# Five tables that interleave the expert blocks with routing and attention, replaced in a macaron layer kernel

## The chip, the core and the metric

One core of a Trainium2 chip. The engines of the core run their own instruction streams side by side: PE (TensorE), DVE (VectorE), ACT (ScalarE), POOL (GpSimd) and SP (SyncE, which only issues DMAs here); they meet at semaphores. The metric is the device time of one execution in microseconds (us), median of the runs.

## What is computed

A macaron layer over 4096 tokens of width 128: half a feed-forward part, windowed attention, and the same feed-forward part by half again, with the same weights both times.

```python
x = x + 0.5 * ffn(layernorm(x))
x = x + attn(layernorm(x))
x = x + 0.5 * ffn(layernorm(x))

def ffn(x):                      # 8 experts, 2 of them for each token, and a shared expert
    normed = layernorm(x) * ln_gamma + ln_beta
    logits = normed @ router_w.T                       # [4096, 8]
    top_v, top_i = top_k(softmax(logits), 2)
    comb = sum(one_hot(top_i) * softmax(top_v))
    for e in range(8):                                 # 2 x 384 hidden columns each
        out += comb[:, e] * swiglu(normed, gate_up_w[e], down_w[e])
    return out + swiglu(normed, shared_gate_up_w, shared_down_w)   # 128 hidden columns

def attn(x):                     # 32 windows of 128 tokens
    q, k, v = x @ Wq.T + bq, x @ Wk.T + bk, x @ Wv.T + bv
    scores = q @ k.T / sqrt(128)
    keep the 32 highest of each row, softmax, times v
    return layernorm(leaky_relu(out) + x) * gamma + beta
```

## The kernel before

The tokens are 32 tiles of 128, taken in 8 steps of 4 tiles. A step of routing is called R: R0 to R7 belong to the first feed-forward part, R8 to R15 to the second. A step of routing normalizes its tokens, forms the logits on PE (`turn_z`, `logits`), picks two experts for each token on DVE (`pick`, then `rows`, which works out a row number for each pair of token and expert), runs the shared expert (`shared_up`, `shared_down` on PE), and scatters every token twice into a list in HBM, sorted by expert (`scatter` on POOL, L1572).

The experts then work on blocks: 128 rows of that list that all belong to one expert. There are 163 blocks, B0 to B162. The lists of the first part come in three groups of 3, 3 and 2 steps (g0, g1, g2), those of the second in two, of 7 steps and 1 (g3, g4), and some groups are listed in several phases; the phases start at B0, B9, B31, B62, B85, B102, B118, B126 and B148. At the start of a phase SP waits for the scatters of all steps up to it. At the end of a group the lists are filled up with zero rows (`fill_all`, two batches of four DMAs at L499, and `fill_spare`). A block consists of parts:

- part 0: SP fetches the 128 rows into `xin` (L479), PE transposes them (L711), ACT writes `x_t` (L920), POOL copies the row numbers to `idx` (L1584);
- part 1: SP copies the expert's gate and up weights (L484), PE multiplies by the gate weights (L716), ACT applies silu (`sil`, L923);
- part 2: PE multiplies by the up weights (L721), DVE forms the product h (L1397);
- part 3: PE multiplies by the down weights (L730), ACT copies (L929), POOL scatters the rows to `results` in HBM (L1589).

Part 4, eight times at the start, transposes the weights of one expert (PE L692). SP reads the row and weight offsets of four blocks at a time into registers (L441). The text writes B83.3 for part 3 of block 83, and h47 for the product of block 47 on DVE.

After the blocks of a group, each of its steps is combined: SP loads the two results of each token (`results(C, ...)`, L515), DVE adds them (`combine`, L1297). With C0 to C7, attention works on the sums of a step: DVE searches for the 32 highest scores (`search`, L1370), forms the `probabilities` (L1385, from ACT's `exps`), PE mixes, and the tokens go on to a routing step of the second part. `TURNS` puts attention step a, the mixing of an earlier one and a routing step into one pass of a loop. The second part's C8 to C14 are combined in the same way and stored; the last step's results are joined at the end (`last_joins`, L1306), after the last block.

Each engine's stream is thus a fixed sequence of routing, attention, filling and combining steps, into which block parts are woven. After every such step the stream calls `turn()`, and a table says how many block parts go there; the order of the parts themselves is fixed by `block_parts`. `WEAVE` (L113 to L131) holds the five tables, one for each engine; `z5` stands for five zeros. What a table does not place, `rest()` emits at the end of the stream:

```python
def __call__(self):
    for _ in range(next(self.counts)):
        self.make(*next(self.parts))
```

Of the kernel before, what the change touches and what calls it, by code (L numbers as in the profile page):

```python
# [97 lines left out]
def turns():  # L98
# [3 lines left out]
    for n, t in enumerate(of):  # L102
# [9 lines left out]

WEAVE = {  # L113
    "sp": """
        8 7 3 8 2 2 13 8 24 12 4 45 9 13 12 1 48 9 7 z1 14 22 38 4 4 z1 1 z1 5 z1 3 z6""",
    "pe": """
        z5 2 2 z1 1 z1 3 z2 1 z1 2 4 2 z2 8 4 3 z2 2 5 4 z1 1 5 2 6 4 z1 6 5 4 z2 98 3 z1 3 6 8 3 z1 5 3 2 3 12 5 z1 5 5 2 5 7 4 4 12 1 22 3 z1 3 z1
        3 3 8 z1 3 z2 6 7 z1 3 2 5 4 2 z1 1 z2 1 z7 1 2 1 z1 3 7 z1 6 1 2 10 5 1 z3 4 9 z1 5 z1 1 5 z3 7 z1 2 3 11 3 3 6 z1 21 5 3 4 z1 22""",
    "act": """
        z12 1 1 z2 1 z1 2 3 z5 1 1 z4 1 6 3 1 z3 1 4 2 2 z4 5 2 z1 3 z3 9 4 2 11 5 56 2 z2 2 3 z1 3 7 z3 3 3 z4 1 4 2 z1 8 z2 1 2 3 1 z4 6 z1 4 4 z1  # L120
        2 z1 2 4 3 z1 1 z2 21 z3 3 2 z1 2 2 z1 5 1 z6 2 z1 2 1 1 4 2 z3 5 2 3 3 z4 1 z2 1 z3 1 1 z15 1 z1 1 1 z1 2 z1 1 z2 8 z1 4 8 z8 1 2 z2 3 2 1
        z2 4 z1 5 3 z6 3 z3 3 8 z4 2 3 3 15 1 z1 1 4 z1 3 40 15 1""",
    "dve": """
        z153 1 z1 1 z4 1 z20 1 z11 1 z4 1 z5 1 z2 1 z9 1 z16 2 z7 2 z2 1 z9 2 z2 1 z13 1 z3 1 1 z1 1 z2 8 1 3 3 1 z2 1 z5 1 z4 1 z1 1 1 z3 1 z6 1 z5
        2 z13 1 z9 1 z2 1 z2 1 z7 1 z5 1 1 z10 2 z25 1 z1 1 z2 1 z10 2 z4 1 z7 1 z15 1 z10 1 z6 2 z9 1 1 z4 1 z9 2 z1 1 z13 2 z5 1 z12 1 z10 1 z2 2
        z20 1 z10 1 z7 2 z4 1 z29 1 z101 1 z3 1 z17 1 z1 1 z3 1 z6 1 z2 1 z10 1 z3 1 z14 1 z17 1 z13 1 z7 1 z15 1 z10 1 z2 1 z46 1 z24 2 z15 1 z5 1
        z8 1 z24 1 z4 2 z19 1 z1 1 z9 2 z1 2 z30 1 2 z10 9 z5 5 z2 2 z2 9 4 1 3 1 1 z1 1 z3 3 z2 1 1 z2 3 z6""",
    "pool": """
        z21 2 1 z1 1 z3 4 z2 3 z1 1 2 z1 5 1 2 2 1 1 3 1 2 z2 1 1 3 3 2 5 16 4 13 4 5 5 z1 5 1 1 2 2 z1 3 z2 2 5 31 z2 3 z1 5 4 z1 2 1 z1 5 1 z3 3
        z10 8 1 7 z1 2 1 1 1 2 2 z3 6 z4 3 z2 1 3 z1 5 5 1 4 2 2 2 z2 3 7 z3 10 7 1 10 3 3 10 40""",  # L130
}  # L131


# [1494 lines left out]
```

## Time and profile before

| | |
|---|---|
| time, median of 3 runs | 658.55 us (658.46 to 661.5) |
| span of the profiled execution | 581.5 us |
| what lies around the span (difference) | 77.05 us |
| instructions | 14497 |
| PE busy | 500.6 us, 86% |
| DVE busy | 388.7 us, 67% |
| ACT busy | 330.0 us, 57% |
| POOL busy | 332.0 us, 57% |

How it is read: the profile page comes from one profiled execution, the times from executions that were not profiled; the span is the time from that execution's first to its last instruction on the core. PEclk is the TensorE clock that was granted, as a share of full speed (0.5 is 1.2 GHz, 1.0 is 2.4 GHz). In the rows of the trace, `[2.30 <-ACT ex L901]` says that the engine stood idle for 2.30 us just before and that the named work ended the wait; `SPq` is SP issuing a DMA.

### The profile page before, as it was taken

The page shows a single profiled execution, that of the slowest core. Times are in us where ns is not written, and L with a number is a line of the kernel's source. Part 1 is how long each engine was busy: PE and PEld are TensorE (multiplying, and loading weights), DVE is VectorE, ACT ScalarE, POOL GpSimd, SP SyncE. Part 2 cuts the span into 40 slices and gives each one's busy share as a digit, 9 for nine tenths or more (in the row PEclk, how much of TensorE's full clock was granted, in tenths as well). Part 3 has the DMA queues.
Part 4 walks back from the last instruction along what each step waited for, and adds up shares of the span by engine and source line. Part 5 has one row for each costly group of instructions (what it writes and reads, how often), then busy time and mean ns, then how long its engine had stood idle before and what let it go on. Part 6 is the DMA issues. An engine that isn't in the chain of part 4 may idle for free.

```text
span 581.5 us, 14497 instructions
## 1 busy us (share of the span) xinstructions
PE 500.6 (86%) x3928; PEld 458.6 (79%) x3928; DVE 388.7 (67%) x1688; ACT 330.0 (57%) x792; POOL 332.0 (57%) x491
## 2 busy tenths in 40 slices
PE   2588999989999989999977499996899999799781
PEld 1466999979899989998974369794889989799780
DVE  5558864732558989879887958999785624222574
ACT  3367556565467777667753357673655546555430
POOL 2273766875565675356674405664566765565542
PEclk9989999999999999999977569997999999999996
DMA  6944858766886554766412254431668767676993
GB/s 184 316 112 167 261 188 237 243 233 239 284 260 218 190 187 173 258 226 205 155 47 59 69 195 176 160 112 54 209 224 257 248 221 246 228 262 237 322 320 124
DMA packets 88012, 117.82 MB, mean 203 GB/s; under 512 B 11848, under 2 KB 60880, under 8 KB 87936
## 3 DMA queue, kind: packets, MB, share of 16 engines
q1 hardware_dynamic: 76208, 96.75, 49.8%
q0 software_dynamic: 9312, 19.16, 9.5%
q10 hardware_dynamic: 2416, 0.99, 0.7%
q8 instruction: 37, 0.61, 0.5%
q14 instruction: 39, 0.32, 0.2%
HBM read 26.57 MB, written 26.19 MB: 91 GB/s over the span
## 4 chain that ended last, share of the span: by engine, by line
PE 52%; SPq 15%; ACT 9%; DMA 7%; issue 7%; DVE 5%; POOL 3%; ACTq 1%; POOLq 0%; DVEq 0%
PE ps_y L730 12%; PE ps_g L716 11%; PE ps_u L721 6%; SPq L441 6%; PE ps_h L721 5%; DMA xin<-rows 5%; SPq L484 4%; SPq L479 3%; PE ps_x L711 2%; PE w L630 2%; SPq L499 2%; POOL rows L1572 2%; ACT zz L849 2%; PE w L660 2%; PE w L616 2%
## 5 line engine op out<-in xcount | busy, mean ns | idle before, releaser
L1589 POOL DMA_INDIRECT results<-raw_gu,idx x163 | 164.6, 1010 | 144.8 <-ACT raw_gu L929 103.1
L1572 POOL DMA_INDIRECT rows<-zz,s_idx x128 | 126.0, 984 | 66.9 <-issue 28.3
L730 PE MATMUL ps_y<-dn_t,raw_gu 128*128 x978 | 139.2, 279 | 5.7 <-ACT raw_gu L929 5.0
L716 PE MATMUL ps_g<-x_t,raw_dn 128*128 128x128 f32 x978 | 137.5, 277 | 0.0
L730 PEld LDWEIGHTS ps_y<-dn_t,raw_gu 128*128 128x128 f32 x978 | 123.4, 193 | 9.3 <-issue 8.5
L716 PEld LDWEIGHTS ps_g<-x_t,raw_dn 128*128 128x128 f32 x978 | 122.8, 192 | 3.6 <-issue 3.5
L929 ACT COPY raw_gu<-ps_y 128x128 f32<-128x128 f32 x163 | 42.9, 263 | 103.5 <-PE ps_y L730 101.8
L923 ACT ACTIVATE sil<-ps_g 128x384 f32<-128x384 f32 x163 | 80.1, 491 | 22.0 <-PE ps_g L716 20.8
L920 ACT ACTIVATE x_t<-ps_x,bf_c,gf_c 128x128 f32<-128x128 f32 x163 | 75.3, 462 | 19.6 <-PE ps_x L711 19.4
L1397 DVE TENSOR_TENSOR raw_gu<-sil,ps_u 128x384 f32<-128x384 f32 x82 | 44.9, 548 | 54.2 <-PE ps_u L721 47.2
L1397 DVE TENSOR_TENSOR raw_gu<-sil,ps_h 128x384 f32<-128x384 f32 x81 | 44.5, 550 | 50.8 <-PE ps_h L721 35.9
L721 PE MATMUL ps_h<-x_t,raw_dn 128*128 128x128 f32 x486 | 68.6, 278 | 2.1 <-DVE raw_gu L1397 2.1
L721 PE MATMUL ps_u<-x_t,raw_dn 128*128 128x128 f32 x492 | 68.9, 276 | 1.3 <-DVE raw_gu L1397 1.3
L721 PEld LDWEIGHTS ps_h<-x_t,raw_dn 128*128 128x128 f32 x486 | 61.6, 194 | 3.9 <-DVE raw_gu L1397 2.5
L721 PEld LDWEIGHTS ps_u<-x_t,raw_dn 128*128 128x128 f32 x492 | 61.7, 192 | 3.1 <-DVE raw_gu L1397 1.5
L711 PE MATMUL ps_x<-ident,xin 128*128 128x128 f32 x163 | 45.4, 279 | 12.3 <-DMA xin<-rows 9.7
L1584 POOL COPY idx<-xin 128x1 int32<-128x1 int32 x163 | 36.5, 225 | 27.6 <-PE ps_x L711 26.8
L849 ACT ACTIVATE zz<-xres,nmr,rstd 128x256 f32<-128x256 f32 x64 | 33.8, 594 | 15.2 <-DVE nmr L1103 14.5
L711 PEld LDWEIGHTS ps_x<-ident,xin 128*128 128x128 f32 x163 | 23.5, 144 | 19.5 <-issue 15.4
L609 PE MATMUL w<-ident,zz 128*128 128x128 f32 x64 | 12.1, 322 | 20.6 <-ACT zz L849 18.3
L1297 DVE TENSOR_TENSOR yg<-yg,gates 128x1024 f32<-128x1024 f32 x15 | 18.3, 1223 | 13.2 <-DMA yg<-results 13.0
L1370 DVE MAX8 top<-wk_s 128x8 f32<-128x128 f32 x96 | 26.4, 283 | 0.0
(172 smaller groups left out, 729.0 us busy)
## 6 DMA issues: line engine op xcount, KB each, us to landing
raw_dn<-gu_t SPq DMA_DIRECT2D x163, 384.0 KB
xin<-rows SPq DMA_DIRECT2D x163, 64.5 KB
yg<-results SPq DMA_DIRECT2D x15, 512.0 KB, 5.1
results<-raw_gu,idx POOLq DMA_INDIRECT x163
rows<-pads SPq DMA_DIRECT2D x40, 64.5 KB
rows<-pads SPq DMA_DIRECT2D x5, 451.5 KB
rows<-zz,s_idx POOLq DMA_INDIRECT x128, 2.4
out<-xres SPq DMA_DIRECT2D x7, 256.0 KB, 3.3
```

The lines of the kernel that those rows point to most:

```text
L711: pe.transpose(ps_x[:, 0, :], xin[:, k4, 0:D], ident[:]).then_inc(xT_ps, 1)
L716: t = pe.matmul(ps_g[k][:, c, :], ws[:, k4, c * P:(c + 1) * P], x_t[:, k, :], start=True, stop=True)
L721: t = pe.matmul(ps_us[k][:, c, :], ws[:, k4, FF + c * P:FF + (c + 1) * P], x_t[:, k, :], start=True, stop=True)
L730: t = pe.matmul(ps_y[:, 0, :], h_t[:, k4, c * P:(c + 1) * P], dn[:, bass.ds(off + c * D, D)], start=(c == 0), stop=(c == FC - 1))
L849: act.activation(zz[R % RING][:, k, :, 0:D], src, ACT.Identity, bias=nmr[:, col + k:col + k + 1], scale=rstd[:, col + k:col + k + 1]).then ...
L920: act.activation(x_t[:, k, :], ps_x[:, 0, :], ACT.Identity, bias=bf_c[:], scale=gf_c[:]).then_inc(xT_sb, 1)
L923: act.activation(sil[:, B % 3, :], ff(ps_g[k]), ACT.Silu).then_inc(sil_done, 1)
L929: act.copy(yb[:, ky, :], ps_y[:, 0, :]).then_inc(y_sb, 1)
L1397: dve.tensor_tensor(h_t[:, k4, :], sil[:, B % 3, :], ff(ps_us[k]), ALU.mult).then_inc(h_done, 1)
L1572: pool.indirect_dma_start(xs, bass.IndirectOffsetOnAxis(s_idx[n][:, c, k:k + 1], 0), zz[n][:, k, c, :], None).then_inc(scat[n], 16)
L1584: pool.tensor_copy(idx[:, ky:ky + 1], xin[:, k4, D:D + 1].bitcast(I32)).then_inc(idx_cp, 1)
L1589: pool.indirect_dma_start(yt, bass.IndirectOffsetOnAxis(idx[:, ky:ky + 1], 0), yb[:, ky, :], None).then_inc(yst[ky], 16)
```

## The change

The texts of the five tables are replaced. Each keeps its number of entries (sp 37, pe 137, act 229, dve 1102, pool 144), so the same steps are followed by a `turn()`; other counts of block parts stand there. The sum of the counts stays at 326 for sp and 163 for dve; it goes from 501 to 480 for pe, 412 to 381 for act and 323 to 261 for pool, and `rest()` emits that much more at the end. No instruction is added or removed, no wait is changed, and within one engine neither the block parts among themselves nor the other steps among themselves change places.

```diff
--- before.py
+++ after.py
@@ -112,22 +112,23 @@
 
 WEAVE = {
     "sp": """
-        8 7 3 8 2 2 13 8 24 12 4 45 9 13 12 1 48 9 7 z1 14 22 38 4 4 z1 1 z1 5 z1 3 z6""",
+        8 4 z1 15 z1 4 12 4 30 6 4 52 2 6 23 z2 59 3 3 10 5 62 2 5 z1 3 z2 1 3 z6""",
     "pe": """
-        z5 2 2 z1 1 z1 3 z2 1 z1 2 4 2 z2 8 4 3 z2 2 5 4 z1 1 5 2 6 4 z1 6 5 4 z2 98 3 z1 3 6 8 3 z1 5 3 2 3 12 5 z1 5 5 2 5 7 4 4 12 1 22 3 z1 3 z1
-        3 3 8 z1 3 z2 6 7 z1 3 2 5 4 2 z1 1 z2 1 z7 1 2 1 z1 3 7 z1 6 1 2 10 5 1 z3 4 9 z1 5 z1 1 5 z3 7 z1 2 3 11 3 3 6 z1 21 5 3 4 z1 22""",
+        z4 1 1 3 1 1 z2 1 z2 1 1 5 2 z2 5 5 6 z2 3 5 2 z2 7 2 6 4 z1 7 4 2 6 2 93 2 z1 3 z1 15 1 z1 4 4 5 3 10 5 z1 5 4 4 3 8 3 3 17 z1 20 3 z1
+        3 z1 3 2 8 z1 2 z2 6 8 z1 4 1 4 5 3 z5 1 z5 1 z1 2 1 z1 3 6 z1 7 1 4 7 7 z2 2 z1 2 7 1 4 1 2 5 z3 5 2 2 3 14 2 2 5 z1 23 2 3 5 z1 1""",
     "act": """
-        z12 1 1 z2 1 z1 2 3 z5 1 1 z4 1 6 3 1 z3 1 4 2 2 z4 5 2 z1 3 z3 9 4 2 11 5 56 2 z2 2 3 z1 3 7 z3 3 3 z4 1 4 2 z1 8 z2 1 2 3 1 z4 6 z1 4 4 z1
-        2 z1 2 4 3 z1 1 z2 21 z3 3 2 z1 2 2 z1 5 1 z6 2 z1 2 1 1 4 2 z3 5 2 3 3 z4 1 z2 1 z3 1 1 z15 1 z1 1 1 z1 2 z1 1 z2 8 z1 4 8 z8 1 2 z2 3 2 1
-        z2 4 z1 5 3 z6 3 z3 3 8 z4 2 3 3 15 1 z1 1 4 z1 3 40 15 1""",
+        z13 4 z3 1 z1 2 1 z4 1 2 z4 2 2 3 4 z4 5 2 z2 1 z1 3 1 6 z4 1 7 4 5 9 6 57 z2 1 4 1 z1 3 6 z1 1 z1 4 1 z4 1 4 2 2 6 z2 1 2 5 z5 3 4 3 3
+        z1 2 z1 3 2 3 z1 2 z2 22 z3 3 2 z1 3 z1 2 3 z2 1 z4 2 z1 2 1 z1 4 3 z3 6 1 3 5 z8 1 z5 1 z13 1 z1 1 1 z1 2 z1 1 z2 9 1 3 6 z1 1 z6 1 2
+        2 z2 3 1 z2 5 2 1 4 z9 1 6 2 8 z3 3 1 z1 17 z1 1 1 4 1 2 12 6 6""",
     "dve": """
-        z153 1 z1 1 z4 1 z20 1 z11 1 z4 1 z5 1 z2 1 z9 1 z16 2 z7 2 z2 1 z9 2 z2 1 z13 1 z3 1 1 z1 1 z2 8 1 3 3 1 z2 1 z5 1 z4 1 z1 1 1 z3 1 z6 1 z5
-        2 z13 1 z9 1 z2 1 z2 1 z7 1 z5 1 1 z10 2 z25 1 z1 1 z2 1 z10 2 z4 1 z7 1 z15 1 z10 1 z6 2 z9 1 1 z4 1 z9 2 z1 1 z13 2 z5 1 z12 1 z10 1 z2 2
-        z20 1 z10 1 z7 2 z4 1 z29 1 z101 1 z3 1 z17 1 z1 1 z3 1 z6 1 z2 1 z10 1 z3 1 z14 1 z17 1 z13 1 z7 1 z15 1 z10 1 z2 1 z46 1 z24 2 z15 1 z5 1
-        z8 1 z24 1 z4 2 z19 1 z1 1 z9 2 z1 2 z30 1 2 z10 9 z5 5 z2 2 z2 9 4 1 3 1 1 z1 1 z3 3 z2 1 1 z2 3 z6""",
+        z141 1 z11 1 z8 1 z7 1 z7 1 z14 1 z4 1 z7 1 z4 1 z15 1 z1 1 z10 2 z3 1 1 z3 1 z8 1 z6 1 z8 1 z1 1 z5 2 z2 15 z1 1 z4 1 z4 1 z5 1 z1 1
+        z3 1 z4 1 z4 1 1 z16 1 z3 1 z5 1 1 z10 1 z5 1 z2 1 z9 2 z23 1 z3 2 z10 2 z5 1 z7 1 z17 1 z11 1 z2 1 z1 1 z3 1 z6 1 z3 1 1 z6 1 z4 1 z8
+        1 z3 1 z5 1 z13 1 z11 1 1 z6 1 z13 1 z9 1 z1 1 z8 1 z4 1 z30 1 z95 1 z7 1 z16 1 1 z4 1 z6 1 z5 1 z7 1 z1 1 z17 1 z16 1 z14 1 z1 1 z4 1
+        z28 1 z1 1 z45 1 z8 1 z6 1 z13 1 z12 1 z4 1 z7 1 z22 1 z7 1 z10 1 z8 1 1 z13 1 z3 2 z8 1 z16 1 z14 1 z1 2 z5 2 z2 32 z4 1 2 z2 2 z2 1
+        z2 2 z6""",
     "pool": """
-        z21 2 1 z1 1 z3 4 z2 3 z1 1 2 z1 5 1 2 2 1 1 3 1 2 z2 1 1 3 3 2 5 16 4 13 4 5 5 z1 5 1 1 2 2 z1 3 z2 2 5 31 z2 3 z1 5 4 z1 2 1 z1 5 1 z3 3
-        z10 8 1 7 z1 2 1 1 1 2 2 z3 6 z4 3 z2 1 3 z1 5 5 1 4 2 2 2 z2 3 7 z3 10 7 1 10 3 3 10 40""",
+        z19 1 1 z4 2 z2 1 z1 4 1 1 1 3 z1 1 1 4 1 z1 2 2 z1 2 z2 1 5 2 z1 4 2 7 5 2 3 7 z1 6 2 3 z1 2 z1 5 z1 1 z1 5 2 1 41 z1 5 1 1 z2 3 4 12
+        z4 2 3 3 2 z9 6 2 1 1 5 1 2 z2 7 z1 2 1 2 z3 1 4 1 z1 2 1 z1 4 1 z1 4 3 5 2 2 z1 2 z1 3 5 z1 1 3 3 6 2 2 4""",
 }
 
 
```

Read as positions, these are the moves that the prediction speaks of. On PE: the transposes of expert 0 go ahead of `prefixes(1)`; B83.3 goes ahead of `turn_z(10)` and B84.3 behind `shared_up(10)`; B85.0 goes ahead of `turn_z(11)`. On SP: the second batch of `fill_all` of g0 goes from behind B6 to ahead of it, that of g2 from after B25.0 to after B23.0; `results(C0)` comes one block later (behind the fetch of B38 instead of B37), `results(C1)` and `results(C2)` two blocks earlier, `results(C3)` two blocks later (from ahead of the fetch of B68 to behind that of B69), `results(C7)` and `fill_spare(3)` ahead of the waits at the start of B85. The batches of g3 stand after B114 and B115 (before: B113 and B117), those of g4 after B122 and B124 (before: B124 and B135); `results(C8)` and `results(C9)` come after part 1 of B155 and B156 (before: B154 and B155). On ACT and DVE: h47 goes ahead of `probabilities` of attention step 0, `x_t` of B56 ahead of `exps` of step 1, h65 and h78 three or more picks later, h72 earlier, h118 behind the block list, and the two combines C8 and C9 ahead of B155.2. On POOL: the scatters of R12 begin earlier, between result scatters.

## Rows read from the trace of the kernel before

**Rows 1.** The page: busy time, and the granted clock in 40 slices.
```profile
PE 500.6 (86%) x3928; PEld 458.6 (79%) x3928; DVE 388.7 (67%) x1688; ACT 330.0 (57%) x792; POOL 332.0 (57%) x491
...
PEclk9989999999999999999977569997999999999996
```
**Rows 2.** The waits of PE: waiting tile, releaser: total us, times, longest.
```profile
PE w L609 <- ACT zz L849: 18.3, 6, 6.3
PE ps_x L711 <- DMA xin<-rows: 9.7, 11, 2.5
```
**Rows 3.** Windows: length, busy of PE, PEld, DVE, ACT, POOL, granted clock, DMA share, GB/s.
```profile
300.00:310.00 10.00, 9.20 (x32) 6.56 (x30) 7.61 (x50) 4.65 (x11) 3.83 (x4) 0.52 0.08 26
...
330.00:340.00 10.00, 5.76 (x25) 4.99 (x26) 6.59 (x36) 5.69 (x13) 0.37 (x2) 0.50 0.59 197
```
**Rows 4.** Timeline of PE at the start (start, duration, instruction, idle before), SP's first fetch.
```profile
25.41 0.21 PE L671 MATMUL w<-sel,upper 128*128 128x40 bf16 x1 [3.55 <-DVE sel L1165]
...
47.52 0.38 SPq L479 DMA_DIRECT2D xin<-rows  x1
```
**Rows 5.** Timeline of SP at the filling of g2: one batch.
```profile
121.04 1.93 SPq L499 DMA_DIRECT2D rows<-pads  x4
```
**Rows 6.** Timeline of PE: the first and the last of four transposes in a row.
```profile
146.39 0.27 PE L711 MATMUL ps_x<-ident,xin 128*128 128x128 f32 x1
...
152.74 0.27 PE L711 MATMUL ps_x<-ident,xin 128*128 128x128 f32 x1
```
**Rows 7.** Timeline at the start of attention: the load of C1, its combine.
```profile
162.81 0.38 SPq L515 DMA_DIRECT2D yg<-results  x1
...
169.37 1.23 DVE L1297 TENSOR_TENSOR yg<-yg,gates 128x1024 f32<-128x1024 f32 x1 [4.14 <-DMA yg<-results]
```
**Rows 8.** Timeline of DVE within the searches: waits for ACT and PE.
```profile
187.37 0.29 DVE L1385 SCALAR_TENSOR_TENSOR pr<-wk_s,ex 128x128 f32<-128x128 f32 x1 [2.30 <-ACT ex L901]
...
217.13 0.55 DVE L1397 TENSOR_TENSOR raw_gu<-sil,ps_h 128x384 f32<-128x384 f32 x1 [1.47 <-ACT sil L923]
...
277.37 0.56 DVE L1397 TENSOR_TENSOR raw_gu<-sil,ps_u 128x384 f32<-128x384 f32 x1 [1.42 <-PE ps_u L721]
```
**Rows 9.** Timeline around the load and the combine of C3.
```profile
236.20 0.40 SPq L515 DMA_DIRECT2D yg<-results  x1
...
242.47 1.21 DVE L1297 TENSOR_TENSOR yg<-yg,gates 128x1024 f32<-128x1024 f32 x1
...
259.49 0.30 DVE L1370 MAX8 top<-sc 128x8 f32<-128x128 f32 x1 [2.91 <-ACT sc L892]
```
**Rows 10.** Timeline in routing steps R9 to R11: down matmuls, waits behind them.
```profile
302.48 1.49 PE L730 MATMUL ps_y<-dn_t,raw_gu 128*128 x6
...
308.88 1.18 PE L730 MATMUL ps_y<-dn_t,raw_gu 128*128 x6
...
312.17 0.69 DVE L1171 TENSOR_TENSOR sh<-sg,w 128x512 f32<-128x512 f32 x1 [2.27 <-PE w L661]
...
336.69 0.45 PE L711 MATMUL ps_x<-ident,xin 128*128 128x128 f32 x1 [1.22 <-DMA xin<-rows]
```
**Rows 11.** The chain that ended last: two fetches of rows, issue to landing.
```profile
333.48 3.07 DMA xin<-rows
...
537.29 5.86 DMA xin<-rows
```
**Rows 12.** Timeline of POOL: its last scatter of R12.
```profile
400.49 0.96 POOL L1572 DMA_INDIRECT rows<-zz,s_idx  x1 [0.30 <-issue]
```
**Rows 13.** Timeline at the filling of g4: DVE at h118, PE behind a batch.
```profile
460.33 0.55 DVE L1397 TENSOR_TENSOR raw_gu<-sil,ps_u 128x384 f32<-128x384 f32 x1 [4.03 <-PE ps_u L721]
...
502.42 0.30 PE L711 MATMUL ps_x<-ident,xin 128*128 128x128 f32 x1 [2.51 <-DMA xin<-rows]
```
**Rows 14.** Timeline at the end: a transpose of PE, the last join of DVE.
```profile
543.29 0.30 PE L711 MATMUL ps_x<-ident,xin 128*128 128x128 f32 x1 [1.58 <-DMA xin<-rows]
...
577.03 2.19 DVE L1306 SCALAR_TENSOR_TENSOR xres<-raw_gu,gates,xres 128x128 f32<-128x128 f32 x8 [5.64 <-DMA raw_gu<-results]
```

## The prediction

> **What bounds the kernel now.** I read the page first: PE is busy 86% of the span, DVE 67%, ACT and POOL 57% [rows 1]. PE is the engine to watch, but 80.9 us of its span are idle (581.5 less 500.6), and part of its busy time is stretched: the granted clock is 0.9 to 1.0 almost throughout and falls to 5 to 7 tenths in five slices, 290 to 365 us, and in slice 27 to 0.6 [rows 1]. The kernel therefore has two faces. Where blocks run undisturbed, four of them follow one another on PE at 2.12 us each (152.74 less 146.39, over three) [rows 6], and no order of the same work gains there. Where attention and routing chains run (150 to 350 us, 365 to 400 us), the DVE chain sets the pace: PE waits 18.3 us in six pieces for the normalized tokens of a routing step, and 9.7 us in eleven for fetched block rows [rows 2]. In the stretch 300 to 310 PE is busy 9.20 us, but at clock 0.52; from 330 to 340 it is busy 5.76 us at 0.50 [rows 3]. Next I read the timelines at each place where the new tables put a part elsewhere. The rows below are those that an altered position can touch. Around the profiled span lie 77.05 us (658.55 less 581.5), which no table touches; I sum against the span and add 77.05, so that a microsecond of span is one of the median.
>
> **The change, part by part.** Instructions, waits and each kind's own order stay. Nothing is removed or added, so a moved step gains only what a wait ahead of it costs, and pays for what it now stands ahead of.
>
> Start. The transposes of expert 0 go ahead of `prefixes(1)`, where PE stood idle for 3.55 us [rows 4]. They fill a hole, but the first block starts when SP issues its fetch at 47.52 [rows 4], after routing, the weights and the list are there. I take -0.5, bounds -1.5 and +0.5.
>
> Fills of g0 to g2. A batch of four DMAs costs SP 1.93 us of issue [rows 5] and its register loads. SP is nearly as loaded as PE while blocks run, so a batch delays the next fetches by up to 2 us. The new places put the g2 batches nearer each other: one wait is gone, another grows. I take 0, bounds -1 and +2.
>
> C0 to C2. `results(C0)` is one block later, one cadence of 2.12 [rows 6]; `results(C1)` is two earlier, about 4.2. DVE waited 4.14 us for the C1 load that SP issued at 162.81 [rows 7]. Both loads gate attention: the later C0 pushes the first search by up to 2.1, the earlier C1 gives back part of that. I take +0.9, bounds -0.3 and +1.5.
>
> Searches 0 to 2. DVE waited 2.30 us for `exps` with h47 queued behind it; now h47 stands ahead and fills the wait. `x_t` of B56 ahead of `exps` shortens the 1.47 us before the product at 217.13 [rows 8]. h65 leaves a wait of like size. Not all is returned, since h47 costs the 0.55 us of such a product wherever it stands [rows 8]. I take -1.8, bounds -2.7 (2.30 plus 1.47, less two products) and 0.
>
> C3. The load was issued at 236.20 and its combine ran at 242.47, without a wait [rows 9]: it was just in time (issue to landing of such loads has a median of 5.1 us on the page's DMA list, left of which is 1.2). Two blocks later is 4.2 later [rows 6], and it lands at about 246. DVE has other parts to do meanwhile, and waited 2.91 us for the scores at 259.49 in any case [rows 9], so part is absorbed. What is queued behind the combine is the routing statistics of R11 and its neighbours and thus attention's next step. I take +2.5, bounds 0 and +4.5. It is the largest cost of the sum.
>
> h72 and h78. h72 goes into a DVE wait; h78 moves behind picks that do not need PE, where DVE waited 1.42 us [rows 8]. I take -1.5, bounds -2 and 0.
>
> R9 to R11. B83.3 and B84.3 are 1.49 and 1.18 us of PE at half clock, ahead of the matmuls on which DVE waited 2.27 us for `shared_up` at 312.17 [rows 10] (and about as long for logits). B83.3 now fills an idle place ahead of `turn_z(10)`; B84.3 stands behind `shared_up(10)`. The chain gains at most 1.49 + 1.18 = 2.67, and what stands ahead of the next steps another 1.9. I take -2.4, bounds -4.5 and 0; the next to be late is the load of C6. `results(C7)` and `fill_spare(3)` go ahead of B85's wait: before, they stood between B85's and B86's fetches, and PE waited 1.22 us [rows 10] for a fetch that took 3.07 from issue to landing [rows 11]. I take -0.5, bounds -1 and +1.
> A fetch behind a load of C8's size took 5.86 us (issued at 537.29), this one 3.07 [rows 11]. The Trainium skill, page "DMA: Bandwidth & Descriptors", section "Queues, rings and completion order", says that on each DMA engine descriptors are consumed in the order of the ring; by it the fetch behind a 512 KB load waits for its share of the load, and moving C7 away would be worth up to 3 us instead of 0.5, the whole time 2.5 less. The row of 3.07 speaks against it here.
>
> R12. POOL's last scatter of R12 began at 400.49 [rows 12], and B102 waited for it; R12's scatters are now interleaved earlier, ending up to 4 us earlier, so that this cover holds even if other parts slip. DVE's end of R12 doesn't move with it. I take -0.5, bounds -3 and +1.
>
> The terms from C0 to here: 0.9 - 1.8 + 2.5 - 1.5 - 2.4 - 0.5 - 0.5 = -3.3.
>
> Fills of g3 and g4. The batches of g3 stand in the middle of blocks: +1.3 at B116. h118 went ahead of the block list and DVE waited 4.03 us there [rows 13]; behind it, the rows and counts of R15 end some 4 us sooner, so g4 can be filled sooner: +1.9 at B125, and at B136, where PE waited 2.51 us behind the batch [rows 13], -3.3 for that wait and a small one next to it. Sum 1.3 + 1.9 - 3.3 = -0.1, bounds -2 and +3.
>
> Tail. C8's load and C9's come one block later, outputs too, and the two combines go ahead of B155.2 on DVE; PE's wait of 1.58 us [rows 14] behind the C8 load moves rather than goes. A combine takes 1.21 us [rows 9]; two of them ahead of a product delay one block by up to 2.4. The end is the last block's scatter, for which the last join had waited 5.64 us [rows 14]. I take +0.9, bounds -1.5 and +4.
>
> Sum: -0.5 + 0 - 3.3 - 0.1 + 0.9 = -3.0. The span becomes 578.5, the time 578.5 + 77.05 = 655.5.
>
> **The rivals.** Forecast: the attention chain keeps its gains, 651.5 to 658.5, chance 0.48.
> Nothing moves, 656 to 661.5, chance 0.20: the DVE chain waits for the C3 load (the +4.5 end), and what was gained ahead of it is gone; in sum 658.55 + 0.5, within 2.5. For it: every chain gain before 242 passes that one load. Against it: the R9 to R11 gains come behind.
> The slow clock closes, 648 to 652.5, chance 0.14: in the routing steps PE works at 0.50 to 0.52 though busy 5.8 to 9.2 of 10 us [rows 3]. With the idle time ahead of B83.3 filled, PE could stay at full clock: of 9.20 us at 300 to 310, half would go (4.6), and from 330 to 340 2.9 of 5.76; this and the gain above give 655.5 - 7.5 + what DVE then holds back, 2.5 = 650.5. Against it: DVE sets that stretch and not PE, and its waits stay.
> The Trainium skill, page "TensorE: Matmul & The Clock Gate", section "Part 1: The HAM clock gate", ties the clock to how busy PE has lately been; by it a denser PE stream ahead of 300 would keep the high clock, which would give this rival's time.
> Slower, 662 to 667, chance 0.18: SP becomes the bound where fills and loads are stacked. One place decides it first, the C3 load: if it lands after 246.5 DVE stands, +4.5 instead of +2.5 (+2); with the same congestion g2's batches cost +2, g3's and g4's +3 in place of -0.1 (+3.1), the tail +4 in place of +0.9 (+3.1). These are 10.2 above 655.5, at most 665.7; it needs over half of it. For it: SP issues eight DMAs and a set of register loads for each four blocks, in about the time PE takes. Against it: the page shows just 9.7 us of PE waiting for fetches [rows 2].
>
> **How the numbers follow.** Predicted is the likeliest, 655.5. Faster by over 0.5% means below 655.26, slower means above 661.84 (0.5%, 3.3 us, is about what a measurement of this kernel can tell from no change). Half of the forecast's 0.48 lies below 655.26: 0.24, and all 0.14 of the clock case: 0.38. Slower: the last rival, 0.18. The rest, 0.24 and 0.20: 0.44. For a range of 8 in 10 I cut at 650.0 (about half of the clock case) and at 662.5 (nearly all of the slower case is above): 0.48 + 0.20 + 0.08 + 0.02 = 0.78, about 0.8.
>
> **What would show it.** DVE's combine of C3 has a wait of 1 to 4 us ahead of it; the wait of 2.30 for `exps` is gone; the waits at R10 (2.27) shrink; PE's waits for fetches at B136 are gone and new ones stand at B116 and B125; the R12 scatters end earlier. The prediction is wrong if the granted clock between 300 and 350 rises to 1.0 (faster), if block cadence grows above 2.12 where batches are stacked (slower), or if DVE's chain has slack that the timelines do not show, in which case no gain arrives.

## The result and the profile after

The kernel after takes 686.36 us (median of 4 runs, 680.09 to 689.03), the kernel before beside it 659.51 us: 1.043 times as long, 95% interval 1.035 to 1.051. Forecast were 655.5 us and a range of 650.0 to 662.5.

The page of the kernel after (busy time and granted clock, answering to [rows 1]; then the engines of the chain that ended last):

```profile
span 683.5 us, 14497 instructions
...
PE 540.1 (79%) x3928; PEld 483.0 (71%) x3928; DVE 391.5 (57%) x1688; ACT 328.8 (48%) x792; POOL 332.5 (49%) x491
...
PEclk9979899888999999998995759997798999999997
...
PE 46%; another core or an unknown queue 13%; ACT 13%; issue 9%; DVE 6%; SPq 5%; DMA 4%; POOL 1%; ACTq 1%; POOLq 0%; DVEq 0%
```

Two things stand here that the profile of before did not have. This profiled execution is itself one of the timed ones: it took 685.24 us, so only 1.74 us lie around its span of 683.5. And 13% of the chain is put down to "another core or an unknown queue", on a program that has one core. The span grew by 102 us over [rows 1], but the time by only 27. So before the two kernels could be compared, the profile of before itself had to be looked at again.

### The profile page after: what moved, and what is told of

Same layout as the page of the kernel before. It is cut to its first block, busy times and chain, and to the rows that moved or that the text cites. A ratio compares the mean times of both kernels' runs of the same rounds, so it can differ in the third digit from the quotient of the medians.

```text
span 683.5 us, 14497 instructions
## 1 busy us (share of the span) xinstructions
PE 540.1 (79%) x3928; PEld 483.0 (71%) x3928; DVE 391.5 (57%) x1688; ACT 328.8 (48%) x792; POOL 332.5 (49%) x491
## 4 chain that ended last, share of the span: by engine, by line
PE 46%; another core or an unknown queue 13%; ACT 13%; issue 9%; DVE 6%; SPq 5%; DMA 4%; POOL 1%; ACTq 1%; POOLq 0%; DVEq 0%
PE ps_y L731 11%; PE ps_g L717 9%; PE ps_h L722 4%; PE ps_u L722 4%; PE w L631 3%; PE w L661 2%; DMA xin<-rows 2%; ACT zz L850 2%; SPq L442 2%; PE ps_x L712 2%; PE w L617 2%; SPq L485 1%; PE w L626 1%; PE w L662 1%
## 5 line engine op out<-in xcount | busy, mean ns | idle before, releaser
L731 PE MATMUL ps_y<-dn_t,raw_gu 128*128 x978 | 145.3, 286 | 44.4 <-ACT raw_gu L930 34.6
L731 PEld LDWEIGHTS ps_y<-dn_t,raw_gu 128*128 128x128 f32 x978 | 127.5, 198 | 56.8 <-issue 56.5
L717 PE MATMUL ps_g<-x_t,raw_dn 128*128 128x128 f32 x978 | 143.6, 285 | 0.0
L717 PEld LDWEIGHTS ps_g<-x_t,raw_dn 128*128 128x128 f32 x978 | 129.1, 201 | 3.4 <-issue 3.2
L921 ACT ACTIVATE x_t<-ps_x,bf_c,gf_c 128x128 f32<-128x128 f32 x163 | 75.3, 462 | 19.4 <-PE ps_x L712 11.4
L722 PE MATMUL ps_h<-x_t,raw_dn 128*128 128x128 f32 x486 | 70.7, 283 | 2.0 <-issue 2.0
L722 PE MATMUL ps_u<-x_t,raw_dn 128*128 128x128 f32 x492 | 71.2, 282 | 0.6 <-issue 0.6
L712 PE MATMUL ps_x<-ident,xin 128*128 128x128 f32 x163 | 46.7, 286 | 25.1 <-DMA xin<-rows 17.2
L722 PEld LDWEIGHTS ps_h<-x_t,raw_dn 128*128 128x128 f32 x486 | 63.8, 199 | 3.4 <-issue 3.4
L722 PEld LDWEIGHTS ps_u<-x_t,raw_dn 128*128 128x128 f32 x492 | 64.7, 199 | 2.1 <-issue 2.0
L631 PEld LDWEIGHTS w<-rw_t,nz_t 128*128 128x128 f32 x128 | 21.3, 252 | 8.1 <-ACT nz_t L876 7.9
L1376 DVE MATCH_REPLACE8 wk_s<-top,wk_s 128x128 f32<-128x128 f32 x96 | 26.6, 281 | 0.0
```

The source lines that it names most:

```text
L631: t = pe.matmul(ps_lg[:, k, :], nz_t[R % 2][:, k, :], rw_t[:], start=True, stop=True)
L712: pe.transpose(ps_x[:, 0, :], xin[:, k4, 0:D], ident[:]).then_inc(xT_ps, 1)
L717: t = pe.matmul(ps_g[k][:, c, :], ws[:, k4, c * P:(c + 1) * P], x_t[:, k, :], start=True, stop=True)
L722: t = pe.matmul(ps_us[k][:, c, :], ws[:, k4, FF + c * P:FF + (c + 1) * P], x_t[:, k, :], start=True, stop=True)
L731: t = pe.matmul(ps_y[:, 0, :], h_t[:, k4, c * P:(c + 1) * P], dn[:, bass.ds(off + c * D, D)], start=(c == 0), stop=(c == FC - 1))
L921: act.activation(x_t[:, k, :], ps_x[:, 0, :], ACT.Identity, bias=bf_c[:], scale=gf_c[:]).then_inc(xT_sb, 1)
```

## A second profile of the kernel before

The first run of the experiments is the unchanged kernel, profiled beside its own times.

> The kernel before, unchanged, for a profile taken beside its own times. Theory U: the 77 us between the span of its profile (581.5) and its median (658.55) are not work around the span but idle pieces within it that its profiled execution did not have: the kernel after has 1.8 us around its span (685.24 less 683.5), so the span here should be about 656.8, with idle pieces of 2 to 6 us on ACT, DVE and PE that no recorded work ends, some 40 to 80 us of them. Rival (mine of the prediction): 77 us lie around the span; then the span is about 581.5 again. Ratio 1.00 in either case.

Measured: 657.64 us (10 runs, 653.51 to 662.38), ratio 0.998 (0.994 to 1.002); the profiled execution took 656.71 us with a span of 654.9. Its page:

```profile
span 654.9 us, 14497 instructions
...
PE 529.6 (81%) x3928; PEld 479.1 (73%) x3928; DVE 389.8 (60%) x1688; ACT 328.5 (50%) x792; POOL 333.0 (51%) x491
...
PEclk9969999797999999999897579696989889999987
...
PE 51%; ACT 13%; another core or an unknown queue 9%; issue 9%; DVE 6%; DMA 5%; SPq 3%; POOL 3%; ACTq 1%; POOLq 0%; DVEq 0%
```

So 1.8 us lie around the span and not 77. The execution on which the prediction rests (span 581.5) was one that no timed run resembles: no timed run of any kernel here was below 641 us, and wherever a timed run has its span on record (190 runs), the span is 1.7 to 2.3 us shorter than the time. The same instructions, with the same busy times on DVE, ACT and POOL, took 73 us more; PE was busy for 29 us more, at a mean granted clock of 0.907 where the first profile had 0.951. All comparisons below are with this second profile. In the views of waits, the kernel before (second profile) and the kernel after have rows of a kind that the first profile had not:

```profile
ACT raw_gu L929 <- remote: 37.6, 14, 6.0
...
DVE raw_gu L1397 <- remote: 25.5, 11, 3.6
...
DVE xres L1197 <- remote: 14.4, 2, 12.4
```

```profile
ACT raw_gu L930 <- remote: 43.5, 15, 6.7
...
DVE raw_gu L1398 <- remote: 25.1, 8, 3.9
...
DVE xres L1198 <- remote: 21.7, 4, 12.6
...
ACT nz_t L876 <- remote: 13.6, 3, 4.8
...
ACT sil L924 <- remote: 12.8, 7, 3.5
```

"Remote" is the view's word for an end of a wait that it can put down to no recorded work. What such a wait is, the timeline shows. First the kernel after, 34 to 47 us:

```profile
34.42 1.16 PE L680 MATMUL w<-sm_t,sh 128*128 128x128 f32 x8 [0.22 <-issue]
...
39.28 0.96 POOL L1573 DMA_INDIRECT rows<-zz,s_idx  x1 [0.30 <-issue]
39.69 0.48 ACT L835 COPY gu_t<-ps_y 128x384 f32<-128x384 f32 x1 [3.77 <-remote]
...
40.22 0.58 PE L693 MATMUL ps_y<-ident,raw_gu 128*128 128x128 f32 x3 [3.64 <-issue]
40.54 0.95 POOL L1573 DMA_INDIRECT rows<-zz,s_idx  x1 [0.30 <-issue]
41.80 0.96 POOL L1573 DMA_INDIRECT rows<-zz,s_idx  x1 [0.31 <-issue]
...
43.07 0.96 POOL L1573 DMA_INDIRECT rows<-zz,s_idx  x1 [0.30 <-issue]
45.36 0.48 ACT L835 COPY dn_t<-ps_g 128x384 f32<-128x384 f32 x1 [5.19 <-remote]
...
46.98 0.69 DVE L1198 SCALAR_TENSOR_TENSOR xres<-w,xres 128x512 f32<-128x512 f32 x1 [12.62 <-remote]
```

PE's `shared_down` (L680) ends at 35.6; DVE, which waits for its semaphore alone, goes on at 46.98, over 11 us later. In the first profile of before the same pair was:

```profile
34.40 1.16 PE L679 MATMUL w<-sm_t,sh 128*128 128x128 f32 x8 [0.96 <-DVE sh L1171]
...
35.59 0.69 DVE L1197 SCALAR_TENSOR_TENSOR xres<-w,xres 128x512 f32<-128x512 f32 x1 [1.25 <-PE w L679]
```

that is, 0.03 us after PE's end. PE's increment of the semaphore arrives late, and it does so while POOL issues one scatter behind another every 1.26 us (16 in a row, from 23.9 to 44.0); it arrives 3 us after that row of scatters has ended. The trace's own record of the semaphore's update stands at 46.96, just before DVE goes on, so it is the increment that is late and not DVE's answer to it.

Increments of ACT and DVE are not seen to be late. Of the waits in the kernel after that an increment of ACT or DVE alone can have ended, 17 of DVE for ACT, 7 of ACT for DVE and 8 of PE for DVE took at most 0.15 us from the end of that work to the start of the next; of 17 of PE for ACT the median is 0.05 us, and the one long one (2.07) is in the first profile of before too. Such waits for PE took up to 11.4 us.

The same was then taken from each trace as a whole: for every PE instruction that increments a semaphore, the time from its end to the start of the ACT or DVE instruction that waits for it, where that engine had been free no later than 0.1 us after PE's end. This is worked out from the timelines and is no view of the profile. By the number of scatters that POOL had issued in the 4 us up to 0.3 us behind PE's end, mean delay in us and number of such pairs:

```
                      1 scatter    2            3            4            sum of delays over 0.5 us
before, first profile 0.04 (60)    0.05 (175)   0.05 (150)   0.04 (20)     2
before, second        0.05 (86)    0.14 (202)   0.67 (60)    3.27 (6)     71
after                 0.03 (102)   0.17 (197)   0.79 (65)    3.16 (5)     83
run d (below)         0.06 (96)    0.14 (180)   1.07 (60)    3.44 (6)     104
```

With one scatter in 4 us the increment takes 0.03 to 0.06 us everywhere. With three or four it is late by 0.7 to 3.3 us on the mean, except in the first profile, where it never is. The sums are rough: pairs in which a product waited for ACT too can be left out or counted, which moves them by up to 11 us. They are also no time of the kernel: the sum of the kernel after is some 12 us above that of the kernel before, its time 27 us.

**Theory R** from here on: in the executions that are timed, PE's semaphore increments are held up while POOL's scatters follow one another closely, and an order of the streams costs or gains by what it does to that. Its rivals: the new positions cost by themselves (S for SP's loads and fills, O for the orders of ACT and DVE), or the late increments come from something else (L).

## Which table costs

Three kernels, each the kernel before with some of its tables exchanged:

```diff
 WEAVE = {
-    "pool": """ ...old... """,      (run d; run b: "sp"; run c: "act" and "dve")
+    "pool": """ ...new... """,
```

> Only SP's table is the new one (fills, loads of results and block fetches at their new places), the four others are the old ones. Theory S: the loss comes from what SP delays (C3 load, stacked fills): most of the 1.043 is here, 1.02 or more. Theory C: the loss comes from the compute engines' orders: 0.995 to 1.01 here. My prediction's terms for SP alone give +0.9 +2.5 -0.5 -0.1 +0.9 = +3.7 us, 1.006.

> Only the tables of ACT and DVE are the new ones; PE, SP and POOL keep the old ones. Theory C: 1.02 or more, as the ACT and DVE orders no longer fit the PE order. Theory S: about 0.995 (my terms for the searches, -1.8 and -1.5, and the tail, give -3.3 to -1 us).

> Only POOL's table is the new one: routing scatters begin earlier between result scatters. Theory P: the earlier scatters hold up the result scatters and through their buffers ACT and the blocks: 1.02 or more. Else within 0.5% (my term was -0.5 us, bounds -3 and +1).

Measured: SP's table 1.011 (1.004 to 1.018), those of ACT and DVE 1.041 (1.033 to 1.050), POOL's 1.041 (1.034 to 1.048). The table of which I had thought least costs as much as all five together. Theory S is out as the main cause; the sum of the three is twice what the kernel after loses, so the costs do not add. POOL's table alone, timeline at 104 to 113 us:

```profile
105.69 0.96 POOL L1572 DMA_INDIRECT rows<-zz,s_idx  x1 [0.30 <-DVE pos L1182]
...
106.10 0.83 PE L730 MATMUL ps_y<-dn_t,raw_gu 128*128 x6
...
107.01 0.98 POOL L1572 DMA_INDIRECT rows<-zz,s_idx  x1 [0.16 <-issue]
...
107.13 3.74 SPq L499 DMA_DIRECT2D rows<-pads  x4
...
108.30 0.95 POOL L1589 DMA_INDIRECT results<-raw_gu,idx  x1 [0.30 <-issue]
...
109.56 0.96 POOL L1572 DMA_INDIRECT rows<-zz,s_idx  x1 [0.30 <-issue]
...
111.70 0.27 ACT L929 COPY raw_gu<-ps_y 128x128 f32<-128x128 f32 x1 [6.24 <-remote]
...
112.21 1.00 PE L730 MATMUL ps_y<-dn_t,raw_gu 128*128 x4 [4.06 <-ACT raw_gu L929]
```

The down matmuls have ended at 106.9, the copy that waits for them starts at 111.70, 1.2 us after the end of the last of five close scatters (the first began at 104.41), and PE then waits 4.06 us for the copy. SP's batch of four DMAs takes 3.74 us here instead of 1.93 [rows 5]. The unchanged kernel in its second profile has slow batches too, of 4.43 and 3.62 us. In this kernel the delays over 0.5 us sum to 104 us, against 71 in the unchanged one. Rows of four or more scatters with less than 1.5 us from one to the next are 26 here, 23 in the kernel after, 18 in the second profile of before, but only 19 with the tables of ACT and DVE alone, which cost as much: how often scatters stand close is not all that counts.

> The new tables on SP, PE, ACT and DVE, and the old one on POOL. In the first four runs the cost of the single swaps did not add up (POOL alone 1.041, ACT and DVE 1.041, all five 1.043). Theory R (back-to-back scatters on POOL hold up PE's semaphore increments): POOL's order alone is worth 4%, so taking it back helps if the rest is neutral; but the ACT and DVE orders alone also gave 1.041, so I expect 1.02 to 1.045. Rival (costs are additive minus my gains; only POOL's part counts): 1.00 to 1.01.

Measured: 1.014 (1.008 to 1.021), below what I had expected. POOL's table carries 2.9 of the 4.3%. Here the delays sum to 74 us, hardly more than in the unchanged kernel, though the tables of ACT and DVE alone (91 us) had cost 4.1%: with PE's and SP's new tables beside them they cost less. PE's table alone was not run.

## Scatters spaced out

If close scatters are the cause, spacing them must give time back, though it adds work to POOL and makes each routing step later:

```diff
+            def lull(n):                     # n small memsets on POOL, each waiting for the last
+                for _ in range(n):
+                    if lulls:
+                        pool.wait_ge(lull_s, len(lulls))
+                    lulls.append(pool.memset(lull_t[:], 0.0).then_inc(lull_s, 1))
...
                         pool.indirect_dma_start(xs, ...).then_inc(scat[n], 16)
+                        lull(3)
                         turn()
```

> The kernel before, with three small memsets (about 0.8 us in all) on POOL behind each of the 128 routing scatters, so that a run of eight scatters is no longer back to back. Added POOL work: about 100 us, beside some 270 us in which POOL idles. Theory R: PE's increments are delivered in the pauses, the unexplained waits of ACT, DVE and PE (some 105 us of clusters over 2 us in this kernel) fall by half or more, and the time falls by 10 to 40 us (0.94 to 0.985). Rival L (late increments come from something else, such as fetches of instructions or SP's DMAs): the waits stay, and the routing chain is longer by 16 x 6 us, partly exposed: 1.00 to 1.05.

> The kernel after with the same pauses. Theory R: it loses most of what sets it apart from the kernel before: within 1% of the kernel before with pauses. Rival S (its order is worse for reasons of its own, such as loads placed too late): it stays 3 to 5% above the kernel before with pauses.

Measured: before with pauses 0.9935 (0.990 to 0.997), after with pauses 0.9925 (0.989 to 0.996), medians 648.11 and 648.39 us. The kernel after, 4.3% slower without pauses, is the equal of the kernel before with them, and both are a little faster than the kernel before. (The ratios are to runs of the kernel before made beside them; its own median was 651.6 us here and 660.2 in the first experiments. A profile was not taken of it each time, so sums of delays are compared across such groups.) POOL in the kernel before with pauses:

```profile
65.53 0.98 POOL L1581 DMA_INDIRECT rows<-zz,s_idx  x1 [0.51 <-issue]
66.52 0.74 POOL L1564 MEMSET lull_t<- 128x128 f32 x3
67.42 0.96 POOL L1581 DMA_INDIRECT rows<-zz,s_idx  x1 [0.16 <-issue]
68.38 0.74 POOL L1564 MEMSET lull_t<- 128x128 f32 x3
```

Scatters start 1.9 us apart instead of 1.26. The delays over 0.5 us fall from 71 to 36 us in the kernel before and from 83 to 44 in the kernel after. In the kernel after with pauses, the waits of ACT that had 43.5 us:

```profile
ACT raw_gu L931 <- remote: 12.2, 7, 3.2
```

My range for the kernel before with pauses was missed on the short side (0.94 to 0.985 expected): the pauses take back what they give elsewhere. PE's waits for fetched rows rise to 48.7 us in the kernel after with pauses (17.2 without), and to 43.5 in the kernel before with pauses (6.5 without):

```profile
PE ps_x L712 <- DMA xin<-rows: 43.5, 19, 8.4
```

This leaves a rival that no run settles. With pauses the chain that ended last runs mainly over POOL in both kernels, where it had 3% of the chain in the kernel before (second profile) and 1% in the kernel after. First before with pauses, then after with pauses:

```profile
POOL 29%; PE 27%; issue 17%; ACT 8%; DMA 7%; DVE 4%; SPq 4%; another core or an unknown queue 2%; ACTq 1%; POOLq 1%; DVEq 0%
```

```profile
POOL 31%; PE 23%; issue 17%; SPq 12%; DMA 8%; ACT 4%; DVE 3%; ACTq 1%; POOLq 1%; another core or an unknown queue 0%; DVEq 0%
```

The pauses thus take away most of the late increments and put a new common bound in their place. That the two kernels then come out equal fits theory R, but it would also come about if POOL's pace hid what the new orders cost by themselves. The control has the same memsets at another place:

```diff
                 pool.wait_ge(ids, R + 1)
                 apart(pool)
+                lull(24)
                 for k in range(TB):
```

> Control for the pauses: the kernel before with the same memsets on POOL (24 for each routing step, about 6 us), but all ahead of the first of its eight scatters, which then run as densely as before. The last scatter of a step comes as late as with spread pauses. Theory R (dense scatters hold up PE's increments): no gain, late increments as in the unchanged kernel (about 70 us in sum) and the 6 us of each step partly exposed: 1.00 to 1.03. Rival (any delay of POOL's routing scatters helps, by the order or by what else it moves): about 0.993, as with spread pauses.

Measured: 1.074 (1.066 to 1.083), more than I had thought; the delays sum to 76 us, as in the unchanged kernel (71). So it is the spacing, not the added work or the later scatters, that removes the late increments. The lump costs 48 us; POOL's `idx` copies, for which SP's fetches wait, stand behind it, and PE's waits for fetched rows are 38.2 us (6.5 in the unchanged kernel). That is no more than the 43.5 us with spread pauses. The two kernels have the same memsets and much the same waits for fetches, but delays of 76 and 36 us, and they lie 8% apart, some 53 us: this pair is the best evidence here that late increments cost time in the kernel before.

Four other sizes and places of the pause:

> The kernel before with the pause of about 0.8 us behind every scatter, routing and result alike (291 pauses, about 230 us of POOL). Theory R: hardly any run of scatters is left, so the fewest unexplained waits; the time is that of the run with routing pauses or lower, unless POOL itself (333 + 230 = 563 us busy) becomes the bound, then 1.0 or above. Rival L: 1.02 or more.

> The kernel after with three memsets behind each routing scatter and one (about 0.25 us) behind each result scatter. Theory R: result scatters that follow one another at once were the late increments that were left (44 us in sum); a third fewer, 640 to 650 us. If POOL becomes the bound, as it did with 0.8 us behind every scatter (1.156), it is above 655 us.

> The kernel after with six memsets (about 1.5 us) behind each routing scatter: scatters of a step come 2.6 us apart. Theory R: hardly a late increment within routing steps (30 us or less in sum), but each step's last scatter comes 11 us later than without pauses; 640 to 660 us. A time above 660 would show that the routing chain, and not only the late increments, sets the time.

> The kernel after with a single memset behind every scatter: the distance of back-to-back scatters grows from 1.26 to about 1.4 us. Theory R: late increments shrink with density, so part of the gain of three memsets (686 to 648): 655 to 680 us. If there is a threshold between 1.4 and 2.0 us, nearly nothing (685); if a small slack is enough, the whole (650).

Measured: 0.8 us behind every scatter of both kinds 1.156 (1.149 to 1.162); 0.8 us behind routing scatters and 0.25 behind result scatters 1.000 (0.996 to 1.004); 1.5 us behind routing scatters 1.127 (1.119 to 1.135); 0.25 us behind all 1.034 (1.023 to 1.046). The second and the third missed what I expected (640 to 650 and 640 to 660 us) with 656.4 and 740.9 us. The first is the purest case of the mechanism: no two scatters are closer than 1.8 us, and the delays over 0.5 us sum to 5 us (500 pairs). Its time fits both what was said for theory R with POOL as the bound (1.0 or above) and rival L (1.02 or more), but the late increments are gone, as theory R alone has it. Its view of waits:

```profile
PEld ps_x L712 <- issue: 143.0, 74, 18.6
PE ps_x L712 <- DMA xin<-rows: 123.0, 56, 17.1
```

POOL is only 68% busy there, but its `idx` copy comes late, SP's next fetch waits for it, and PE for the fetch. In the kernel with 1.5 us the same wait is 135.4 us. Here POOL sets the time (59% of the chain that ended last) with hardly a late increment. A pause of 0.25 us changes the density little: the delays sum to 80 us (83 without), and 1.034 against 1.043 is within the intervals.

## Where the new orders cost

In POOL's new table 92 of its block parts come ahead of the last scatter of R7 (old: 115), and 42 ahead of that of R5 (old: 47): the scatters of R4 to R7 stand between fewer result scatters. (With the `turn()` right behind that scatter it is 93 and 146, 49 and 63, the numbers of the expectation below.) Two kernels have the new table on one side of R7's last scatter and the old one on the other (the count at the joint makes up the difference); a third is the kernel after with the first half old again.

> The kernel before with POOL's new table only up to the scatters of R7; from there on the old one. In this part the new table has 93 block parts of POOL behind it when R7 is scattered (old: 146), and only 49 after R5 (old: 63): the scatters of R4 to R7 stand more densely among result scatters, and 53 block parts follow in one piece. Theory R: most of POOL's 4.1% is here, 1.02 to 1.035. Rival (it is the R8 to R15 part, where attention waits for each step): 1.00 to 1.01.

> The other half alone: POOL's old table up to R7, the new one from R8. Theory R: 1.005 to 1.02, as in the run with the whole new POOL table the blocks from B61 on lost 13 of 31 us against the unchanged kernel. Rival: 1.03 or more.

> The kernel after with POOL's old table up to R7. Theory R: it recovers what that half costs, 2 to 3 of the 4.3%: 1.01 to 1.025 against the kernel before.

Measured: first half 1.020 (1.016 to 1.024), second half 1.016 (1.011 to 1.020), together near the whole table's 1.041; delays some 93 to 104 and 82 to 85 us, by how the pairs are chosen, against 71. The kernel after with the first half old: 1.036 (1.030 to 1.041), delays 85 to 103 us. It recovers only 0.7 of the 2%, and my expectation (1.01 to 1.025) was wrong: what one half costs depends on the other streams. The transposes of single blocks (start in us, from the timelines) show that the loss comes in steps all over the kernel:

```
                 B0   B16  B30  B50  B61  B84  B110 B162
before, second   62   125  169  222  262  333  489  635
POOL's new       62   136  176  246  280  356  517  666
after            63   133  178  243  275  355  520  664
```

Last, the pauses in four routing steps only (`lull(3 if R < 4 else 0)`), and the pauses with the tables of ACT and DVE:

> The kernel before with the pauses of 0.8 us only behind the 32 scatters of R0 to R3. With pauses behind all 128, the gain against the unchanged kernel was 4 us at B0 and 9 us at B16 and stayed about so to the end. Theory R: the same gain from a quarter of the pauses, 0.985 to 0.995. If the later pauses paid too, it is smaller: 0.995 to 1.00.

> The kernel after with pauses in R0 to R3 only. In the kernel before these gave the whole gain. Theory R: what the new order adds lies in R4 to R15 as well, where the scatters are not spaced here; so only some 10 of the 38 us come back: 1.02 to 1.035. If it is near 0.9925, as with pauses in all steps, the new order's cost lies in the first four steps alone.

> The new tables on ACT and DVE only (1.041 without pauses), with the pauses of 0.8 us behind all routing scatters. Theory R: the cost of these two tables also comes by late increments, so it is gone with the pauses: 0.99 to 1.00. Rival O (their order costs by itself, as the products and copies come in another order than PE delivers them): it stays 2 to 4% above the 0.9935 of the kernel before with pauses.

Measured: 0.992 (0.989 to 0.996) for the kernel before: the whole gain of 128 pauses by 32 of them. 1.019 (1.008 to 1.031) for the kernel after, a little better than expected, where pauses in all steps gave 0.9925: so of the 5.1% that all pauses give back, 2.4 come from R0 to R3 and 2.7 from R4 to R15. 1.018 (1.008 to 1.028) for ACT and DVE with pauses in all steps: the delays fall from 91 to 35 us, but against the 0.9935 of the kernel before with pauses 2.4% stay (1.018 / 0.9935), of 4.1% without pauses. So theory R explains 1.7 of the 4.1%, and rival O, as far as the wide interval tells, the larger part for these two tables: the two orders without PE's new one cost time by themselves. The fastest kernels of all are these three with pauses (before in R0 to R3, before and after in all steps), 0.992 to 0.9935 of the kernel before; their intervals overlap.

## The prediction, step by step

**The 77.05 us around the span: wrong, and the step from which the miss follows.** The step reads "Around the profiled span lie 77.05 us (658.55 less 581.5), which no table touches". The second profile shows 1.8 us around a span of 654.9: the rest was idle time and slower work within the span, which the first profiled execution alone did not have, 71 us of late increments in sum (not all of them on the path) and 29 us more of PE's busy time. I had both numbers before me, a span of 581.5 and a lowest run of 658.46, and took the difference to be a constant that the tables cannot touch. What the tables changed could not be read from that profile. Every term of the sum was priced on a timeline in which PE's increments arrive in 0.04 us.

**POOL's order: wrong.** Taken at -0.5 us with bounds of -3 and +1 (the R12 term), it costs 27 us alone. I asked only whether the last scatter of a step comes earlier, not what stands around it. With the old POOL table the other four cost 1.4%, with the new one 4.3%.

**The searches, C0 to C2 and R9 to R11: the waits got shorter, in part by name only.** PE's waits for normalized tokens, 18.3 us [rows 2] and 18.8 in the second profile, are 6.9 in the kernel after; DVE's for loaded results 13.3 and 5.6 (and 2.9 more for which no releaser is named); the one for `exps` is 1.84 us at 241.53, in the second profile 4.5. In the kernel after:

```profile
PE w L610 <- ACT zz L850: 6.9, 2, 3.7
...
DVE yg L1298 <- DMA yg<-results: 5.6, 5, 2.1
```

These are some 21 us less of waits (11.9, 7.7 and 1.8; the waits for `exps` sum to 4.5 and 2.7), and no time was gained by them. One of them has only changed its name. The prediction had no term for B85.0 going ahead of `turn_z(11)` on PE. In the second profile of before PE waits there for the tokens and takes B85's transpose behind them:

```profile
375.45 1.12 PE L609 MATMUL w<-ident,zz 128*128 128x128 f32 x4 [6.34 <-ACT zz L849]
376.36 0.42 PE L711 MATMUL ps_x<-ident,xin 128*128 128x128 f32 x1
```

In the kernel after the transpose comes first, and PE waits for its fetch, which SP issues when the scatters of R10 have landed:

```profile
397.28 0.96 POOL L1573 DMA_INDIRECT rows<-zz,s_idx  x1 [0.30 <-issue]
...
401.00 0.35 SPq L480 DMA_DIRECT2D xin<-rows  x1
...
402.90 0.45 PE L712 MATMUL ps_x<-ident,xin 128*128 128x128 f32 x1 [9.11 <-DMA xin<-rows]
```

So 6.34 of the 11.9 us stand as 9.11 under another name. With the pauses in both kernels the two come out equal (648.1 and 648.4 us), so my sum of -3.0 us, 0.5%, is not confirmed even there; the difference of the two is within their intervals.

**C3: mechanism right, its place in the sum of no weight.** The combine has the forecast wait ahead of it:

```profile
299.00 1.23 DVE L1298 TENSOR_TENSOR yg<-yg,gates 128x1024 f32<-128x1024 f32 x1 [2.49 <-issue]
```

2.49 us, in the range of 1 to 4. "Issue" means only that the view names nothing that ended it; SP had issued the load at 293.50, 5.5 us before, and such loads took 5.1 us in the first profile, so that the load may well have ended it. What the wait cost the kernel no run shows.

**The fills and SP's table: perhaps too low.** My terms for SP come to +3.7 us; measured is 1.011, some 7 us, and its interval (3 to 12) holds 3.7. In the kernel after, PE's waits for fetches rise from 6.5 to 17.2 us, but 9.1 of them are the one ahead of B85, which comes from PE's table and from the late scatters of R10. The waits that I named at B116 and B125 are not there (0.42 us and none).

**The tail: right, as far as one profile of each kernel tells.** From the transpose of B154 to the end of the span it is 43.9 us in the second profile of before and 44.9 in the kernel after, +1.0 for the +0.9 of the sum, and the last join waits for 5.72 us, where it was 5.64 in [rows 14] and 5.78 in the second profile:

```profile
678.99 2.19 DVE L1307 SCALAR_TENSOR_TENSOR xres<-raw_gu,gates,xres 128x128 f32<-128x128 f32 x8 [5.72 <-DMA raw_gu<-results]
```

**The rival on the clock: fell.** The mean granted clock is 0.902 after and 0.907 in the second profile of before; the low stretch among routing steps [rows 3] is there in both pages. **The slower rival** named SP and had 665.7 us as its end; the sign was right, the mechanism was not the main one (SP alone 1.011), and the place that I gave for the decision, the C3 load, shows a wait of 2.49 us and no more.

**A reading that was off.** The five slices with a clock of 5 to 7 tenths, 290 to 365 us, are four, 291 to 349 us, and slice 27 (from 0) has 0.7, not 0.6 [rows 1]. No term of the sum uses them.

**What stays open.** What holds PE's increments back is not shown, only when: the runs do not tell POOL's issuing of a scatter from the scatter's packets in flight. The ends of PE's instructions are modelled in a profile, so the traces do not tell a late increment from a result of PE that is written late either. Why one profiled execution of the kernel before ran without the delays is open, too. Its scatters stand closer, if anything (165 distances under 1.5 us, in the second profile 142), so closeness alone does not bring the delays. Its trace has as many records of semaphore updates as the program has increments (3831 for 3814), the second only 2762 and that of the kernel after 2821; whether increments were delivered together or records were lost is not shown. How much of the 27 us comes by late increments, and how much by the new orders themselves, is open: the delays grow by only 12 us, the tables of ACT and DVE keep 2.4% with the pauses, and the equality of both kernels with pauses has the rival named above. And the costs of the tables are not additive, so which single move costs how much can't be read from these runs.

## What to carry to other kernels

Compare the span of a profile with the time of the same execution before building on it; if tens of us lie between the profile and the timed runs, the profile shows another kind of execution, and a second profile comes before any sum. Where a program keeps scatters on POOL going, the distance between them is a cost of its own: ask of every reordering how many scatters it puts in a row, and not only when the last is done. Gains read from single waits, 21 us of them here, are worth nothing if the new order meets a limit that the profile did not show, or if the wait only comes back on another row. And an experiment that takes one cause away can put another bound in its place: look at the chain of its profile before two equal times are read as a proof.

## What the runs showed of the hardware

A PE semaphore increment reached its waiting engine in 0.04 us (median) where POOL had issued at most one scatter in the 4 us before; with three it took 0.67 to 1.07 us on the mean and with four 3.2 to 3.4 us, the longest over 11 us during 16 scatters in a row. This was so in three traces of kernels without pauses, and not in the first profile of the kernel before (0.05 and 0.04 us). In the kernel after, where this was looked at, increments of ACT and DVE were in time (0.15 us or less from the end of DVE's work, a median of 0.05 us from ACT to PE). With no two scatters closer than 1.8 us PE's increments were nearly all in time (5 us of delay in a whole kernel), at 1.26 us they were not. Pausing 0.8 us behind 32 of the 291 scatters made the kernel 0.8% faster; pausing behind all of them made it 15.6% slower, with POOL busy for only 68% of the span.
